# Last block's v repeated in float32, its z written to the buffer of p, and VectorE's scalar reads placed behind the issue of that z

## The chip, the cores and the metric

The kernel runs on one core of one Trainium2 chip. The metric is device time in microseconds (us) of one execution. Below, TensorE is PE in the rows (PEld are its weight loads), VectorE is DVE, ScalarE is ACT, GpSimd is POOL and SyncE is SP; DVEq is VectorE's sequencer, the part that reads registers and issues instructions.

## The reference

A graph layer over 53125 edges between 3125 nodes with 32 features each, and a layer norm of the sum:

```python
r = edge_vec / norm(edge_vec);  sh1 = sqrt(3) * r
xs, xd = x[edge_src], x[edge_dst]
s1 = concat(xs[:, :8], xd[:, :8]);  v1 = concat(xs[:, 8:], xd[:, 8:]) as (E, 16, 3)
w  = relu(emb @ fc1_w1) @ fc1_w2          # four (16, 8) matrices per edge
vdot1 = einsum('euk,ek->eu', v1, sh1) / sqrt(3)
s_t = a1 * (s1 . Wss + vdot1 . Wvv);  v_t = a1 * ((s1 . Wsv) sh1 + v1 . Wvs)
w2 = relu(emb @ fc2_w1) @ fc2_w2          # six (8, 8) matrices per edge
# the same once more with s_t, v_t and w2 gives scal, gates, vecs
edge_out = concat(tanh(scal), vecs * tanh(gates)) * edge_weight
x = layernorm(x + segment_sum(edge_out, dst))
```

The edges come sorted by destination, with many per node.

## The kernel before

The edges are padded and cut into NB = 104 blocks of BE = 512 edges, four tiles of 128. Blocks are counted from 0, so block 103 is the last. All engines run the same written-out loop `for i in STEPS` over i = -5 to 104; at step i each engine does one stage each for several blocks. The order of work on each engine is the order in which this loop is written, and semaphores order the engines against each other. There is no scheduler.

The stages that matter here, for a block k:

- `first_layer(k)` on TensorE: four float32 products, each over 32 rows, into PSUM banks 0 to 3 (line L1073 in the rows).
- `products(k)` on VectorE (L751): those four banks times the hidden layer `h1`, into the buffer `p_s`.
- `sum_1(k)` on TensorE (L986): four column groups of `v_ps` (bank 7) from `p_s`. It is v of this block.
- v is then split in three bfloat16 parts that sum to the float32 value, in place: ScalarE copies `v_ps` to the bfloat16 tile `v_s` (`part_of_v(k, 0)`, L528), TensorE takes the first of these away from the groups that hold later parts (`less_part(k, 0)`, L993), ScalarE copies again, TensorE again, ScalarE a third time. This way group 0, 1 and 2 of `v_s` come to hold the three parts.
- `repeat(k)` on TensorE (L1029): four bfloat16 products with the selection matrix `rep_m` repeat v into banks 0 to 3, each over 32 rows.
- `products2(k)` on VectorE (L791): those banks times the second hidden layer `h2`, into the buffer `z_s`.
- `sum_2(k)` on TensorE (L1004), a copy to `u_r` on ScalarE (`copy_u`, L500), and `turn(k)` on TensorE (L1053), four transposes into bank 7 (bank 0 for the last block).
- `gates(k)`, `gate_sums(k)` on VectorE (L802, L805, L807; L811, L814), `tanhs(k)` on ScalarE (L482), `gated(k)` and `outputs(k)` on VectorE (L773, L778), `over_nodes(k)` on TensorE (L1021), `accumulate(k)` on VectorE (L766).

`accumulate(k)` adds a window of 42 columns at an offset that is the block's first destination node. The offset is read from SBUF into a register of VectorE's sequencer by `base_of(k)` (L757); one such read is a TENSOR_LOAD, two register operations and an assertion. The flag of L852 (has any block more than a window of nodes) is read in the same way. In the loop there is one such read each step, written behind `products2`. Behind the loop VectorE's program reads

```python
            o, a, b, c, d = range(NB - 5, NB)
            flag = dve.value_load(misfits[0:1, 0:1], min_val=0, max_val=EP)
            bases_of = {k: base_of(k) for k in (o, a, b)}
            gated(a)
            outputs(a)
            gates(b)
            products2(d)
            gate_sums(b)
```

so o is block 99 and a, b, c, d are blocks 100 to 103. When all blocks are added, 16 products on TensorE take the mean away (L1159), and VectorE and ScalarE do the layer norm.

Of the kernel before, what the change touches and what calls it, by code (L numbers as in the profile page):

```python
# [9 lines left out]
ALU = mybir.AluOpType  # L10
# [37 lines left out]
def program(nc, xp, xt, src_t, dst_t, dst_rows, base_col, bases_row, emb, vec_t, wgt, w1, w2a, w2b, out):  # L48
    ctx = ExitStack()
    with ctx:  # L50
        def sb(name, shape, dt=F32):
            return ctx.enter_context(nc.sbuf_tensor(name, shape, dt))

        def sem(name):
            return ctx.enter_context(nc.semaphore(name))
# [16 lines left out]
        sel_g = sb("sel_g", [128, 4, 8])  # L72
        of_group = sb("of_group", [128, 4])
        of_part = sb("of_part", [128, 4])
        sum_m = sb("sum_m", [128, 4, 8])
        rep_m = sb("rep_m", [128, 4, 16, 8], BF16)
        less = [sb(f"less{n}", [128, 128], BF16) for n in range(2)]
# [35 lines left out]
        z_s = sb("z_s", [128, 4, BE])  # L113
        u_r = [sb(f"u{n}", [128, BE]) for n in range(2)]
        v_s = sb("v_s", [128, BE], BF16)
        m1 = sb("m1", [128, T, 4, 16])
        m2 = sb("m2", [128, T, 2, 16])
        gsc = sb("gsc", [128, T, 16])
# [73 lines left out]
        setup_step = sem("setup_step")  # L192
        consts_ready = sem("consts_ready")
        rep_step = sem("rep_step")
        misfit_parts = sem("misfit_parts")
        misfit_sum = sem("misfit_sum")
        misfits_ready = sem("misfits_ready")
# [69 lines left out]
        def real(m):  # L267
            return 0 <= m < NB
# [210 lines left out]
        def _(act):  # L479
# [109 lines left out]
            for i in STEPS:  # L589
                if real(i):  # L590
                    hidden_2(i)
                if real(i):
                    part_of_v(i, 0)
                if real(i + 1):
                    hidden_1(i + 1)
                if real(i):
                    part_of_v(i, 1)
                if i == -1:
                    act.wait_ge(n2_ready, 2)
                    nc.scalar.activation(nrm_t[:, TA:TILES], n2_t[:, TA:TILES], ACT.Sqrt).then_inc(norm_ready, 1)  # L600
                if real(i + 3) and i < 2:
                    copy_sources(i + 3)
                if real(i + 3):
                    copy_rows(i + 3)
                if real(i + 3) and i >= 2:
                    copy_sources(i + 3)
                if real(i + 4):
                    copy_one_hot(i + 4)
                if real(i + 4) and i + 4 >= 1:
                    copy_oht(i + 4)  # L610
                if real(i):
                    part_of_v(i, 2)
                if real(i - 3):
                    tanhs(i - 3)
                if real(i - 1):
                    copy_u(i - 1)
                if real(i + 2):
                    copy_f(i + 2)
                later_emb(i)
# [15 lines left out]
        def _(dve):  # L635
# [89 lines left out]
            link(nc.vector.tensor_reduce(of_group[:], ident[:].rearrange("p (g c) -> p g c", g=4), AX.X, ALU.add))  # L725
            link(nc.vector.tensor_reduce(of_part[:], ident[:].rearrange("p (g n c) -> p n g c", g=4, n=4), AX.XY, ALU.add))
            nc.vector.tensor_scalar(less[1][:], ident[:], of_part[:, 2:3], -1.0, ALU.mult, ALU.mult).then_inc(rep_step, 1)
            link(nc.vector.tensor_tensor(of_part[:, 0:1], of_part[:, 0:1], of_part[:, 1:2], ALU.add))
            link(nc.vector.tensor_tensor(of_part[:, 1:2], of_part[:, 1:2], of_part[:, 2:3], ALU.add))
            link(nc.vector.tensor_tensor(of_part[:, 0:1], of_part[:, 0:1], of_part[:, 2:3], ALU.add))  # L730
# [5 lines left out]
            def late_constants():  # L736

                dve.wait_ge(weights_loaded, 48)
                link(nc.vector.tensor_scalar(w_z[:], w_z[:], c2, None, ALU.mult))
                nc.vector.tensor_scalar(w_z[:, 0, 16:24], w_z[:, 0, 16:24], SQRT3, None, ALU.mult).then_inc(weights_ready, 1)  # L740
                nc.vector.tensor_copy(iota[:], iota_i[:]).then_inc(consts_ready, 1)
                dve.wait_ge(dst_loaded, 16)
                nc.vector.tensor_copy(dst_f[:], dst_i[:]).then_inc(place_ready, 1)
                nc.vector.memset(acc[:], 0.0).then_inc(acc_zeroed, 1)
                link(nc.vector.tensor_reduce(strip_sum[:], ident[:].rearrange("p (g c) -> p c g", g=4), AX.X, ALU.add))
                nc.vector.tensor_scalar(centre[:], strip_sum[:], -1.0 / D, None, ALU.add).then_inc(consts_ready, 1)

            def products(m):
                dve.wait_ge(g_done, m + 1)
# [38 lines left out]
            def products2(k):  # L788
                dve.wait_ge(rep_done, k + 1)
                dve.wait_ge(h2_ready, k + 1)  # L790
                nc.vector.tensor_tensor(z_s[:], ps[:, 0:4, :], h2_r[k % 3][:].unsqueeze(1).to_broadcast([128, 4, BE]),  # L791
                                        ALU.mult).then_inc(z_done, 1)

            def gates(k):
# [21 lines left out]
            for i in STEPS[:-1]:  # L816
                if real(i):
                    products(i)
                if real(i - 3):
                    gates(i - 3)  # L820
                if real(i - 1):
                    products2(i - 1)
                if real(i - 5):
                    base = base_of(i - 5)
                if real(i - 4):
                    gated(i - 4)
                if real(i - 5):
                    accumulate(i - 5, base)
                if real(i - 3):
                    gate_sums(i - 3)  # L830
                if real(i - 4):
                    outputs(i - 4)
                if real(i + 2):
                    sum_along(i + 2)
                if i == 0:
                    late_constants()

                for step, at_step in enumerate((-2, -2, 0, 0, 0, 1, 1, 1)):
                    if i == at_step:
                        if step >= 1 and step != 2:  # L840
                            dve.wait_ge(r4_step, step if step < 2 else step - 1)
                        ins = directions(step, TA, TILES)
                        if step == 1:
                            ins.then_inc(n2_ready, 1)
                        elif step == 7:
                            ins.then_inc(r4_ready, 1)
                        else:
                            ins.then_inc(r4_step, 1)


            o, a, b, c, d = range(NB - 5, NB)
            flag = dve.value_load(misfits[0:1, 0:1], min_val=0, max_val=EP)  # L852
            bases_of = {k: base_of(k) for k in (o, a, b)}
            gated(a)
            outputs(a)
            gates(b)
            products2(d)
            gate_sums(b)
            gates(c)
            gated(b)  # L860
            gate_sums(c)
# [73 lines left out]
        def _(pe):  # L935
# [59 lines left out]
            def sum_2(k):  # L995
                pe.wait_ge(z_done, k + 1)
                if k == 0:
                    pe.wait_ge(weights_ready, 4)
                    pe.wait_ge(consts_ready, 3)
                pe.wait_ge(h1_ready, min(k + 3, NB))  # L1000
                if k + 2 >= NB:
                    pe.wait_ge(u_ready, k)
                for g in range(4):
                    last = nc.tensor.matmul(s2_ps[32 * g:32 * g + 32], w_z[:, min(g, 1), :], z_s[:, g, :],  # L1004
                                            start=True, stop=True)
                last.then_inc(s2_done, 1)

# [17 lines left out]
            def repeat(k):  # L1025
# [4 lines left out]
                                            start=True, stop=True)  # L1030
                last.then_inc(rep_done, 1)

            def rows(m):
                pe.wait_ge(window_loaded[m % 3], 16 * (m // 3 + 1))
                pe.wait_ge(oht_copied, m + 1)
                if m == 1:
                    pe.wait_ge(rows_copied, 1)
                if m >= 2:
                    pe.wait_ge(f_copied, m - 1)
                for t in range(T):  # L1040
                    last = nc.tensor.matmul(rows_ps[:, t, :], oht_r[m % 2][:, TE * t:TE * t + TE], window_r[m % 3][:],  # L1041
                                            start=True, stop=True)
                last.then_inc(rows_done, 1)

            def turn(k):
                pe.wait_ge(u_ready, k + 1)
                bank = 0 if k == NB - 1 else 7
                if k < NB - 1:
                    pe.wait_ge(v_step, 3 * min(k + 3, NB))
                if 1 <= k < NB - 1:  # L1050
                    pe.wait_ge(e_free, k)
                for t in range(T):
# [40 lines left out]
            for i in STEPS:  # L1093
                if i == -4:
# [3 lines left out]
                    pe.wait_ge(misfits_ready, 1)  # L1098
                    flag = pe.value_load(misfits[0:1, 0:1], min_val=0, max_val=EP)
                    spread_places(0)  # L1100
                if real(i - 1):
                    repeat(i - 1)
                if real(i):
                    hidden_2(i)
# [10 lines left out]
                    pe.wait_ge(misfits_ready, 1)  # L1115
                if real(i + 1):
                    hidden_1(i + 1)
                if real(i):
                    less_part(i, 0)
                if real(i + 1):  # L1120
                    first_layer(i + 1)
                if real(i + 4) and i + 4 >= 1:
                    spread_places(i + 4)
                if real(i):
                    less_part(i, 1)
                if i == NB:
                    turn(i - 2)
                if real(i - 1):
                    sum_2(i - 1)
                if real(i - 2) and i < NB:  # L1130
                    turn(i - 2)
                if real(i + 2):
                    turn_features(i + 2)
# [82 lines left out]
```

## Time and profile before

| | |
|---|---|
| median of 3 runs | 744.84 us (744.56 to 747.78) |
| the profiled execution | 744.64 us, of which 742.8 us is the span of the trace |
| busy, share of the span | PE 93%, DVE 93%, ACT 75%, POOL 71% |
| chain that ended last | PE 87%, DVE 4% |

The span is counted from the first to the last instruction in the trace; 1.84 us of the execution lie around it. Times in the rows are us from the start of the span unless they say ns. "x8" is the number of instructions merged in a row; a float32 product counts as two. The bracket at the end of a timeline row gives the engine's idle time before it and what ended it.

### The profile page before, as it was taken

The numbers are of one execution on the slowest core, as the hardware profiler recorded it, in microseconds if no ns is written. First come the engines' busy times: TensorE is split into PE (matmuls) and PEld (weight loads), VectorE is DVE, ScalarE is ACT, GpSimd is POOL, SyncE is SP. The second block draws the span as 40 slices with busy tenths as digits, with TensorE's granted clock in tenths as the row PEclk, the third lists the DMA queues.
The fourth block names the chain that finished last, engine by engine and source line by source line (L and its number), as shares of the span: only waits on it lengthen the run. The fifth ranks groups of instructions, "written<-read, shape, count | busy, mean of one in ns | idle before, by whom it ended". The sixth has DMA issues, their size and how long they took to land.

```text
span 742.8 us, 19328 instructions
## 1 busy us (share of the span) xinstructions
PE 687.2 (93%) x5990; PEld 282.9 (38%) x5990; DVE 691.7 (93%) x1231; ACT 560.2 (75%) x1281; POOL 528.0 (71%) x653
## 2 busy tenths in 40 slices
PE   2359999999999999999999999999999999999984
PEld 2113334434443444344344444334434443444321
DVE  7488999999999999999999999999999999999986
ACT  3238887887888778888888888877788888878752
POOL 5676888778876887688768886787778876887200
PEclk7569999999999999999999999999999999999998
DMA  5412211111111211121112111211121111111000
GB/s 132 112 34 47 47 32 28 40 46 28 30 42 27 50 26 42 28 47 31 43 26 45 29 43 27 48 31 27 40 46 29 28 39 26 41 27 27 20 1 23
DMA packets 45822, 28.49 MB, mean 38 GB/s; under 512 B 23299, under 2 KB 43941, under 8 KB 45721
## 3 DMA queue, kind: packets, MB, share of 16 engines
q1 hardware_dynamic: 31402, 19.43, 9.9%
q0 software_dynamic: 13312, 6.84, 6.0%
q8 instruction: 52, 0.85, 0.5%
q10 hardware_dynamic: 1006, 0.96, 0.5%
q14 instruction: 50, 0.40, 0.2%
HBM read 22.46 MB, written 4.74 MB: 37 GB/s over the span
## 4 chain that ended last, share of the span: by engine, by line
PE 87%; DVE 4%; issue 2%; ACT 1%; POOL 1%; DVEq 0%; ACTq 0%
PE ps L1073 16%; PE ps L986 14%; PE ps L1004 13%; PE ps L993 9%; PE ps L1053 8%; PE ps L974 6%; PE ps L1029 5%; PE ps L1066 4%; PE ps L1060 3%; PE ps L964 3%; PE ps L1041 3%; PE ps L948 2%; PE ps L1021 2%; DVE p_s L751 2%; ACT v_s L528 1%
## 5 line engine op out<-in xcount | busy, mean ns | idle before, releaser
L374 POOL DMA_INDIRECT xs<-in_xp,src_i x416 | 401.0, 964 | 115.2 <-issue 104.3
L751 DVE TENSOR_TENSOR p_s<-ps,h 128x2048 f32<-128x2048 f32 x104 | 238.3, 2292 | 21.6 <-PE ps L1073 20.9
L791 DVE TENSOR_TENSOR z_s<-ps,h 128x2048 f32<-128x2048 f32 x104 | 237.6, 2284 | 1.3 <-PE ps L1029 1.2
L528 ACT CAST v_s<-ps 128x512 bf16<-128x512 f32 x312 | 182.2, 584 | 48.3 <-PE ps L986 43.2
L1073 PE MATMUL ps<-f,w_f 32*128 32x512 f32 x832 | 119.7, 642 | 4.3
L986 PE MATMUL ps<-p_s,sum_m 128*32 128x512 f32 x832 | 111.7, 605 | 0.6 <-DVE p_s L751 0.5
L1004 PE MATMUL ps<-z_s,w_z 128*32 128x512 f32 x832 | 110.8, 605 | 1.5 <-DVE z_s L791 1.5
L494 ACT COPY f<-ps 128x512 f32<-128x512 f32 x104 | 61.0, 587 | 41.9 <-PE ps L974 41.5
L993 PE MATMUL ps<-v_s,less 128*128 128x512 bf16 x208 | 81.1, 390 | 2.8 <-ACT v_s L528 2.6
L416 POOL TENSOR_TENSOR along<-fe,r 128x192 f32<-128x192 f32 x104 | 54.2, 521 | 32.8 <-ACT fe L506 26.3
L1053 PEld LDWEIGHTS ps<-ident,u 128*128 128x128 f32 x416 | 43.8, 141 | 87.6 <-issue 87.0
L534 ACT ACTIVATE h<-ps 128x512 f32<-128x512 f32 x104 | 62.2, 598 | 19.7 <-PE ps L1060 12.4
L540 ACT ACTIVATE h<-ps 128x512 f32<-128x512 f32 x104 | 62.2, 598 | 13.7 <-PE ps L1066 8.5
L488 ACT ACTIVATE oht<-ps 126x512 bf16<-126x512 f32 x104 | 62.5, 601 | 11.1 <-POOL e_part L397 5.3
L500 ACT COPY u<-ps 128x512 f32<-128x512 f32 x104 | 61.1, 588 | 12.4 <-PE ps L1004 2.1
L1053 PE MATMUL ps<-ident,u 128*128 128x128 f32 x416 | 68.0, 286 | 1.3 <-DVE m L807 1.0
L974 PE MATMUL ps<-ident,fe 128*128 128x128 f32 x416 | 63.5, 276 | 5.9 <-ACT ohs L523 5.7
L993 PEld LDWEIGHTS ps<-v_s,less 128*128 128x128 bf16 x208 | 19.9, 96 | 89.9 <-ACT v_s L528 78.5
L417 POOL TENSOR_TENSOR fe<-fe,r 128x192 f32<-128x192 f32 x104 | 54.0, 519 | 0.0
L974 PEld LDWEIGHTS ps<-ident,fe 128*128 128x128 f32 x416 | 49.2, 143 | 8.7 <-issue 7.3
L1021 PEld LDWEIGHTS ps<-ohs,eo_all 128*32 128x32 f32 x832 | 25.1, 108 | 68.0 <-issue 65.5
L1073 PEld LDWEIGHTS ps<-f,w_f 32*128 32x128 f32 x832 | 35.3, 185 | 34.2 <-issue 34.2
(129 smaller groups left out, 848.7 us busy)
## 6 DMA issues: line engine op xcount, KB each, us to landing
emb<-e_dram SPq DMA_DIRECT2D x309, 30.0 KB
xs<-in_xp,src_i POOLq DMA_INDIRECT x416
e_dram<-e_part SPq DMA_DIRECT2D x7, 360.0 KB, 3.0
e_in<-in_emb SPq DMA_DIRECT2D x8, 240.0 KB, 2.9
window<-x_dram SPq DMA_DIRECT2D x104, 7.9 KB
eo_all<-in_vec_t SPq DMA_DIRECT2D x1, 528.0 KB, 5.0
x_dram<-eo_all SPq DMA_DIRECT2D x1, 525.0 KB
place<-place_dram SPq DMA_DIRECT2D x26, 20.0 KB
```

The source lines that it names most:

```text
L374: nc.gpsimd.indirect_dma_start(xs_r[n][:, t, :], None, xp, bass.IndirectOffsetOnAxis(src_i[:, m * T + t:m * T + t + 1], axis=0)).then_inc( ...
L488: nc.scalar.activation(oht_r[m % 2][:], oht_ps, ACT.Relu).then_inc(oht_copied, 1)
L528: nc.scalar.copy(v_s[:], v_ps).then_inc(v_step, 1)
L534: nc.scalar.activation(h1_r[m % 2][:], h1_ps, ACT.Relu, scale=1.0 / math.sqrt(10.0)).then_inc(h1_ready, 1)
L751: nc.vector.tensor_tensor(p_s[:], ps[:, 0:4, :], h1_r[m % 2][:].unsqueeze(1).to_broadcast([128, 4, BE]), ALU.mult).then_inc(p_done, 1)
L791: nc.vector.tensor_tensor(z_s[:], ps[:, 0:4, :], h2_r[k % 3][:].unsqueeze(1).to_broadcast([128, 4, BE]), ALU.mult).then_inc(z_done, 1)
L974: last = nc.tensor.transpose(f_ps[:, TE * t:TE * t + TE], fe_r[m % 2][:, t].rearrange("p g c -> p (g c)"), ident[:])
L986: last = nc.tensor.matmul(v_ps[32 * g:32 * g + 32], sum_m[:].rearrange("p n c -> p (n c)"), p_s[:, g, :], start=True, stop=True)
L993: nc.tensor.matmul(v_ps, less[n][:], v_s[:], start=False, stop=True, skip_group_check=True).then_inc(s1_step, 1)
L1004: last = nc.tensor.matmul(s2_ps[32 * g:32 * g + 32], w_z[:, min(g, 1), :], z_s[:, g, :], start=True, stop=True)
L1053: last = nc.tensor.transpose(ps[:, bank, TE * t:TE * t + TE], u_r[k % 2][:, TE * t:TE * t + TE], ident[:])
L1073: last = nc.tensor.matmul(ps[:, g, :], w_f[32 * g:32 * g + 32], f_r[m % 2][32 * g:32 * g + 32], start=True, stop=True)
```

## The change

The constants get one more selection matrix, `rep_last`, in float32 (128 x 16 x 8). It is built in two steps: `first_copy` in VectorE's setup, and the broadcast of it in step 6 of the loop (`select_last`). For block 103 alone, ScalarE copies `v_ps` once, to the float32 tile `v_last`; the two further parts and the two `less_part` products fall away. `repeat(103)`, which stood at the start of step 104, is replaced by `repeat_last` in step 103: four float32 products with `rep_last` and `v_last`, behind `turn(101)` and ahead of `sum_2(102)`. Its result times `h2` goes to `p_s` in place of `z_s`. On VectorE, `gates(101)` and `products2(103)` move ahead of the four scalar reads, the reads stand right behind `products2(103)`, and `gated(100)` and `outputs(100)` behind the reads, with the first gate sum of block 101 between them.

```diff
@@ ScalarE
-                if real(i):
+                if i == NB - 1:
+                    act.wait_ge(s1_step, 3 * i + 1)
+                    nc.scalar.copy(v_last[:], v_ps).then_inc(v_last_copied, 1)
+                elif real(i):
                     part_of_v(i, 0)
...
-                if real(i):
+                if real(i) and i < NB - 1:
                     part_of_v(i, 1)
...
@@ VectorE
             nc.vector.tensor_scalar(less[1][:], ident[:], of_part[:, 2:3], -1.0, ALU.mult, ALU.mult).then_inc(rep_step, 1)
+            link(nc.vector.tensor_scalar(first_copy[:], sel_w[:], of_part[:, 0:1], None, ALU.mult))
...
+            def select_last():
+                dve.wait_ge(rep_step, 6)
+                nc.vector.tensor_copy(rep_last[:], first_copy[:].unsqueeze(1).to_broadcast([128, 16, 8])).then_inc(last_selected, 1)
...
-                nc.vector.tensor_tensor(z_s[:], ps[:, 0:4, :], h2_r[k % 3][:].unsqueeze(1).to_broadcast([128, 4, BE]),
+                z = p_s if k == NB - 1 else z_s
+                nc.vector.tensor_tensor(z[:], ps[:, 0:4, :], h2_r[k % 3][:].unsqueeze(1).to_broadcast([128, 4, BE]),
...
-            flag = dve.value_load(misfits[0:1, 0:1], min_val=0, max_val=EP)
-            bases_of = {k: base_of(k) for k in (o, a, b)}
-            gated(a)
-            outputs(a)
             gates(b)
             products2(d)
+            bases_of = {k: base_of(k) for k in (o, a, b)}
+            flag = dve.value_load(misfits[0:1, 0:1], min_val=0, max_val=EP)
+            gated(a)
             gate_sums(b)
+            outputs(a)
             gates(c)
@@ TensorE
+            def repeat_last():
+                pe.wait_ge(z_done, NB - 1)
+                pe.wait_ge(v_last_copied, 1)
+                pe.wait_ge(last_selected, 1)
+                for g in range(4):
+                    last = nc.tensor.matmul(ps[:, g, :], rep_last[32 * g:32 * g + 32].rearrange("p j c -> p (j c)"),
+                                            v_last[32 * g:32 * g + 32], start=True, stop=True)
+                last.then_inc(rep_done, 1)
...
             def turn(k):
-                if k < NB - 1:
-                    pe.wait_ge(v_step, 3 * min(k + 3, NB))
+                if k < NB - 3:
+                    pe.wait_ge(v_step, 3 * (k + 3))
+                elif k < NB - 1:
+                    pe.wait_ge(v_last_copied, 1)
...
-                if real(i - 1):
+                if real(i - 1) and i < NB:
                     repeat(i - 1)
...
-                if real(i):
+                if real(i) and i < NB - 1:
                     less_part(i, 1)
-                if i == NB:
+                if i >= NB - 1:
                     turn(i - 2)
+                if i == NB - 1:
+                    repeat_last()
                 if real(i - 1):
                     sum_2(i - 1)
-                if real(i - 2) and i < NB:
+                if real(i - 2) and i < NB - 1:
                     turn(i - 2)
```

What this makes of the order on TensorE, from the sum of v of block 103 (`ps<-p_s,sum_m`) to the sum of its z. Before:

```order
L986 MATMUL ps<-p_s,sum_m 32x512 x4
L1021 MATMUL ps<-ohs,eo_all 32x42 x4
L993 MATMUL ps<-v_s,less 128x512 x2
L1004 MATMUL ps<-z_s,w_z 32x512 x4
L1053 MATMUL ps<-ident,u 128x128 x4
L1029 MATMUL ps<-v_s,rep_m 128x512 x4
L1021 MATMUL ps<-ohs,eo_all 32x42 x4
L1053 MATMUL ps<-ident,u 128x128 x4
L1004 MATMUL ps<-z_s,w_z 32x512 x4
L1090 MATMUL ps<-xt_n,centre 32x400 x2
```

After; line numbers have moved, and `less_part` is gone, the transposes and the repeat of block 103 stand ahead of `sum_2(102)`, and the sum of its z reads `p_s`:

```order
L1002 MATMUL ps<-p_s,sum_m 32x512 x4
L1037 MATMUL ps<-ohs,eo_all 32x42 x4
L1080 MATMUL ps<-ident,u 128x128 x4
L1054 MATMUL ps<-v_last,rep_last 128x512 x4
L1020 MATMUL ps<-z_s,w_z 32x512 x4
L1037 MATMUL ps<-ohs,eo_all 32x42 x4
L1080 MATMUL ps<-ident,u 128x128 x4
L1020 MATMUL ps<-p_s,w_z 32x512 x4
```

So the products ahead of the repeat are now four transposes and no longer two `less_part`, the eight halves of `sum_2(102)` and the transposes.

On VectorE, from the last `outputs` of the loop (block 99) on, before:

```order
L778 TENSOR_TENSOR eo_all<-m_1,eo_all 128x4x3x8
L852 TENSOR_LOAD misfits
L852 ISA x2
L757 TENSOR_LOAD bases
L757 ISA x2
L757 TENSOR_LOAD bases
L757 ISA x2
L757 TENSOR_LOAD bases
L757 ISA x2
L773 TENSOR_TENSOR eo_all<-eo_all,wgt_s 128x4x16
L778 TENSOR_TENSOR eo_all<-m_0,eo_all 128x4x3x8
L802 TENSOR_TENSOR m<-ps,r 128x96
```

and after:

```order
L791 TENSOR_TENSOR eo_all<-m_1,eo_all 128x4x3x8
L816 TENSOR_TENSOR m<-ps,r 128x96
L819 TENSOR_TENSOR m<-ps,r 128x256
L821 TENSOR_TENSOR m_1<-m,ps 128x96
L805 TENSOR_TENSOR p_s<-ps,h_1 128x2048
L770 TENSOR_LOAD bases
L770 ISA x2
L770 TENSOR_LOAD bases
L770 ISA x2
L770 TENSOR_LOAD bases
L770 ISA x2
L871 TENSOR_LOAD misfits
```

The four reads (L852 and L757 before, L770 and L871 now) have moved from ahead of the gates of block 101 to behind the z of block 103 (`p_s<-ps,h_1` at L805), and `gated(100)` with them.

## Rows read from the trace of the kernel before

**Rows 1.** The page: the chain that ended last, and the costliest group of VectorE

```profile
PE 87%; DVE 4%; issue 2%; ACT 1%; POOL 1%; DVEq 0%; ACTq 0%
...
L751 DVE TENSOR_TENSOR p_s<-ps,h 128x2048 f32<-128x2048 f32 x104 | 238.3, 2292 | 21.6 <-PE ps L1073 20.9
```

**Rows 2.** By stretch: PE, PEld, DVE, ACT, POOL busy (count), TensorE's clock, DMA, GB/s

```profile
716.00:724.00 8.00, 5.61 (x55) 2.12 (x51) 5.85 (x14) 3.74 (x8) 0.00 (x0) 1.00 0.00 0
724.00:733.00 9.00, 5.91 (x68) 2.49 (x68) 7.11 (x26) 2.82 (x6) 0.00 (x0) 1.00 0.02 4
733.00:743.00 10.00, 1.66 (x18) 0.42 (x16) 4.42 (x12) 1.21 (x3) 0.00 (x0) 0.80 0.13 40
```

**Rows 3.** Timeline of TensorE, end of the kernel: start, us, instruction, idle before

```profile
713.81 1.14 PE L1073 MATMUL ps<-f,w_f 32*128 32x512 f32 x8
...
719.86 0.39 PE L993 MATMUL ps<-v_s,less 128*128 128x512 bf16 x1 [0.62 <-ACT v_s L528]
...
721.25 1.06 PE L1004 MATMUL ps<-z_s,w_z 128*32 128x512 f32 x8
722.25 0.66 PE L1053 MATMUL ps<-ident,u 128*128 128x128 f32 x4
722.84 0.40 PE L1029 MATMUL ps<-v_s,rep_m 32*128 32x512 bf16 x4
...
726.58 1.06 PE L1004 MATMUL ps<-z_s,w_z 128*32 128x512 f32 x8 [1.48 <-DVE z_s L791]
...
728.36 0.66 PE L1053 MATMUL ps<-ident,u 128*128 128x128 f32 x4
...
731.26 0.28 PE L1021 MATMUL ps<-ohs,eo_all 128*32 128x42 f32 x8 [1.15 <-DVE eo_all L778]
...
733.11 1.55 PE L1159 MATMUL ps<-acc,centre 128*32 128x400 f32 x16
```

**Rows 4.** Timeline of VectorE, end of the kernel

```profile
715.01 2.29 DVE L751 TENSOR_TENSOR p_s<-ps,h 128x2048 f32<-128x2048 f32 x1 [0.44 <-PE ps L1073]
...
717.87 2.28 DVE L791 TENSOR_TENSOR z_s<-ps,h 128x2048 f32<-128x2048 f32 x1
...
720.77 0.28 DVE L778 TENSOR_TENSOR eo_all<-m,eo_all 128x96 f32<-128x96 f32 x1
723.14 0.23 DVE L773 TENSOR_TENSOR eo_all<-eo_all,wgt_s 128x64 f32<-128x64 f32 x1 [2.08 <-issue]
723.40 0.29 DVE L778 TENSOR_TENSOR eo_all<-m,eo_all 128x96 f32<-128x96 f32 x1
723.58 0.25 DVE L802 TENSOR_TENSOR m<-ps,r 128x96 f32<-128x96 f32 x1
...
724.24 2.29 DVE L791 TENSOR_TENSOR z_s<-ps,h 128x2048 f32<-128x2048 f32 x1
726.44 0.28 DVE L811 TENSOR_TENSOR m<-m 128x128 f32<-128x128 f32 x1
...
728.15 0.29 DVE L778 TENSOR_TENSOR eo_all<-m,eo_all 128x96 f32<-128x96 f32 x1
...
729.39 0.26 DVE L802 TENSOR_TENSOR m<-ps,r 128x96 f32<-128x96 f32 x1 [0.87 <-PE ps L1053]
```

**Rows 5.** Timeline of ScalarE, end of the kernel

```profile
719.22 0.59 ACT L528 CAST v_s<-ps 128x512 bf16<-128x512 f32 x1 [0.52 <-PE ps L986]
```

**Rows 6.** VectorE's sequencer, the flag read, then a base read in the loop (durations in ns)

```profile
L852 DVEq TENSOR_LOAD <-misfits x1: 310/310/310, 720.6 to 720.6; - x1
...
L757 DVEq TENSOR_LOAD <-bases x1: 306/306/306, 717.8 to 717.8; - x1
```

**Rows 7.** Timeline of VectorE, in the setup

```profile
27.82 0.37 DVE L785 TENSOR_REDUCE fe<-along 128x64 f32<-128x192 f32 x1 [2.90 <-POOL fe L417]
```

**Rows 8.** In the setup: a stretch as in rows 2, and TensorE's timeline in it

```profile
34.00:36.00 2.00, 1.38 (x13) 0.93 (x17) 0.00 (x0) 0.88 (x2) 1.70 (x2) 0.50 0.17 26
...
35.49 2.09 PE L1073 MATMUL ps<-f,w_f 32*128 32x512 f32 x8
```

More of the change, by code:

```diff
@@ L74, in program @@
         of_part = sb("of_part", [128, 4])
+        first_copy = sb("first_copy", [128, 8])
         sum_m = sb("sum_m", [128, 4, 8])
@@ L115, in program @@
         v_s = sb("v_s", [128, BE], BF16)
+        v_last = sb("v_last", [128, BE])
+        rep_last = sb("rep_last", [128, 16, 8])
         m1 = sb("m1", [128, T, 4, 16])
@@ L194, in program @@
         rep_step = sem("rep_step")
+        last_selected = sem("last_selected")
+        v_last_copied = sem("v_last_copied")
         misfit_parts = sem("misfit_parts")
@@ L834, in _ @@
                     sum_along(i + 2)
+                if i == 6:
+                    select_last()
                 if i == 0:
@@ L1003, in sum_2 @@
                 for g in range(4):
-                    last = nc.tensor.matmul(s2_ps[32 * g:32 * g + 32], w_z[:, min(g, 1), :], z_s[:, g, :],
+                    last = nc.tensor.matmul(s2_ps[32 * g:32 * g + 32], w_z[:, min(g, 1), :], (p_s if k == NB - 1 else z_s)[:, g, :],
                                             start=True, stop=True)
@@ L1117, in _ @@
                     hidden_1(i + 1)
-                if real(i):
+                if real(i) and i < NB - 1:
                     less_part(i, 0)
@@ L1123, in _ @@
                     spread_places(i + 4)
-                if real(i):
+                if real(i) and i < NB - 1:
                     less_part(i, 1)
-                if i == NB:
+                if i >= NB - 1:
                     turn(i - 2)
+                if i == NB - 1:
+                    repeat_last()
                 if real(i - 1):
                     sum_2(i - 1)
-                if real(i - 2) and i < NB:
+                if real(i - 2) and i < NB - 1:
                     turn(i - 2)
```

## The prediction

> **What bounds the kernel now.** I read the page first. Its chain gives TensorE 87% of the span, and VectorE sat idle ahead of the product of `p_s` for 21.6 us over 104 blocks, 0.21 us a block, waiting for TensorE [rows 1]. So the loop runs at TensorE's pace, and the change takes nothing from the loop. It works on the last 25 us, which I read next in the table by stretch: from 716 to 733 us TensorE is busy 11.5 us of 17 and VectorE 13.0, so both wait for something [rows 2]. What for stands in the two timelines.
>
> On TensorE the three-part split of v of block 103 runs from 719.22, where ScalarE takes the first copy, and its products are spaced by ScalarE's copies (first `less_part` at 719.86) [rows 3, 5]. Then follow `sum_2(102)` at 721.25, the transposes of block 101 at 722.25 and the repeat at 722.84, over at 723.24 [rows 3]. But the z of block 103 starts only at 724.24 [rows 4]. VectorE is the later of the two: its last `outputs` of the loop starts at 720.77, and the next work at 723.14, with 2.08 us idle put down to issue [rows 4]. That is the four scalar reads: the first starts at 720.6 [rows 6], so they hold VectorE 723.14 - 720.6 = 2.5 us, or 0.62 us each. Behind them come `gated(100)`, `outputs(100)` and the gates of block 101, 1.10 us to the z. From the z on everything hangs on VectorE and on the way back over TensorE: sum of z at 726.58, transposes of block 103 at 728.36, `gates(103)` at 729.39 [rows 3, 4]. At that last place two more reads are in the way: they begin beside the `outputs` at 728.15, and 2 x 0.62 gives 729.39, the start seen [rows 4]. The row names TensorE as the releaser, but its transposes ended at 729.02 [rows 3]. From 729.39 to the end the program is the same before and after.
>
> **When z can start after the change, TensorE's side.** ScalarE's copy of `v_ps` to float32 has the shape of the copy at 719.22, which took 0.59 us whatever it writes here; I take 719.81. TensorE followed that copy at 719.86 [rows 3, 5]. Now the transposes of block 101 start there, and the repeat follows 722.84 - 722.25 = 0.59 us behind, at 720.45 [rows 3]. The four float32 products over 32 rows were never run at this place; `first_layer` is the same form (32x512, eight instructions). There VectorE started 715.01 - 713.81 = 1.20 us after the first of them [rows 3, 4]. So z can start at 721.65. The wait for the z of block 102 costs nothing: that z started at 717.87 and is over at 720.15 [rows 4].
>
> **VectorE's side.** `outputs(99)` starts at 720.77 and holds 0.18 us (723.40 to 723.58), the gates of a block hold 0.66 (723.58 to 724.24) [rows 4]: ready at 721.61. Both sides meet at 721.65, so neither a cheaper repeat nor cheaper gates alone would give more. z starts 724.24 - 721.65 = **2.59 us earlier**.
>
> **What the reads cost behind the issue of z.** In the loop a read stands right behind z: it starts at 717.8 with z at 717.87 [rows 4, 6], so reads run beside the product. The four take 2.5 us from 0.05 ahead of z's start. z gives way to its successor after 726.44 - 724.24 = 2.20 [rows 4]. VectorE goes on 2.45 after z's start, **0.25 us late**. If the reads fit entirely, this is 0; if they started only with z's end, it is 2.50 (a rival below). I take 0.25, since the row shows the overlap of one, and the other three are the same instructions.
>
> Where z has to wait for TensorE, the reads may start earlier than z. The Trainium skill (Perfetto Trace Analysis, DVE / Act Engine Instruction) says that the sequencer pushes an instruction into a wait queue and is then ready for the next. By that rule the reads would start at z's push and not at its start, and the sum would gain up to 0.25 more; by the row, which shows 0.07 us between them, it would not. The trace leaves it open, since nothing there waits long enough; the page is not used in the sum.
>
> **What is put between z and `gates(103)`.** `gated(100)` and `outputs(100)`, once ahead of z, now lie behind it. They held 723.58 - 723.14 = 0.44 us together [rows 4]: **0.44 us back**. With the first gate sum between them part of the gap is filled, so 0.3 is the lower bound. Their readers are `over_nodes(100)` on TensorE, behind the transposes of block 103, and those come later anyway.
>
> **What is late next.** `sum_2(102)` now stands behind the repeat, near 721.5 in place of 721.25. From a `sum_2` to its transposes is 728.36 - 726.58 = 1.78, so those of block 102 run from 723.3 to 723.95, and VectorE wants them for `gates(102)` at about 724.9. The sum of z of block 103 follows z's start by 726.58 - 724.24 = 2.34, at 723.99, just behind them; its transposes follow at 725.77 and end at 726.43 [rows 3]. `gates(103)` on VectorE's side comes at 729.39 - 2.59 + 0.25 + 0.44 = 727.49. So TensorE has 1.06 us to spare there, and VectorE with its reads is the bound of this stretch.
>
> **Edits at nothing.** `first_copy` is one small instruction in VectorE's setup, behind which VectorE idles 2.90 us for GpSimd [rows 7]; uncovered it would cost some 0.3. `select_last` is one copy in step 6, of about 0.2 us, against the 0.21 us that VectorE idles in a block [rows 1]; uncovered 0.2. Two copies less on ScalarE and two products less on TensorE free nothing beyond the times above. Writing z to `p_s` is the same instruction, and its reader `sum_1(103)` is done long before.
>
> **Sum.** -2.59 + 0.25 + 0.44 = -1.90. The profiled execution took 744.64, so 742.74; it lies 0.20 below the median of the runs, so the median to expect is **742.9**. The bounds: 2.3 us gained with the reads hidden and `outputs` at 0.3, some 0.95 gained with the repeat at its dearest row.
>
> **Rivals.**
> *The float32 repeat is dear, or another place holds the tail.* Products of this form took 2.09 us at 1.2 GHz [rows 8], 0.95 more than at 2.4. TensorE's clock was at full speed from 716 to 733 [rows 2] and now idles less ahead of the repeat, which speaks against; a switch of shapes that costs, or a tail bound that I do not see, would look the same. Gain 0.95, 743.9. Chance 0.14.
> *The reads are not hidden.* They start with z's end: 2.50 in place of 0.25, and the sum is -2.59 + 2.50 + 0.44 = +0.35: 745.2. For it: before, four in a row held the engine 2.5 us. Against: the single read in the loop starts beside z [rows 4, 6], and VectorE does not idle behind that z. Chance 0.06.
> *Slower: the clock falls.* TensorE waits for `outputs(102)` ahead of its last node products, 1.15 us before [rows 3]. Its transposes of block 103 now end 2.59 earlier and that `outputs` 1.90, so it waits about 1.8. If the clock fell to 1.2 GHz there, the work from 731.26 to 734.66 would take 3.4 us more: 744.84 + 3.4 - 1.9 = 746.3. It decides once over half of that work runs at 1.2. Against: the clock held 1.00 over an idle time of 1.48 us [rows 2, 3], and the mean of 0.80 from 733 to 743 means that it fell some 4 us before 743, at 739, over 4 us after TensorE's last product. The Trainium skill (TensorE: Matmul & The Clock Gate, The HAM clock gate) likewise has an idle TensorE drop to 1.2 GHz; no row here shows it at waits this short. Chance 0.05.
> *The change does nothing measurable*, since added constants or moved addresses cost in the loop what the end gives: 744.8. No row speaks for it. Chance 0.07.
>
> **How the numbers follow.** The forecast has 0.68: a gain of 1.4 to 2.4 us, so 742.4 to 743.4. The range of 8 in 10 is **741.8 to 744.8**: it takes in the dear repeat and the hidden reads, and allows for the runs' own spread, which reached from 0.28 below to 2.94 above the median before. Half a per cent, about what a measurement of this kernel can tell from no change, is 3.7 us. No case reaches 741.1 or 748.6; for what I have missed I leave 0.03 for faster and 0.03 for slower, and 0.94 lies within.
>
> **What would show it right or wrong.** From the first product of `sum_1(103)` on, z of block 103 should start 2.6 us earlier than before, and `gates(103)` should follow it by 5.15 + 0.69 = 5.84 us in place of 5.15. The first repeat product should stand 0.6 us behind the first transpose. The repeat should take 1.1 us; TensorE should not be the bound at `gates(103)`; no idle of more than 0.3 us should stand behind z; the clock should read 1.00 to 733. The loop should take the same time a block. A wrong prediction would come from a wait for the transposes of block 102, from the reads, or from the clock.

## The result, and the profile after

The changed kernel took 743.05 us (median of 14 runs), the kernel before 746.22 (14 runs, timed together); the ratio is 0.9961 with a 95% interval of 0.9943 to 0.998. That is 2.9 us of gain, with 1.5 to 4.3 inside the interval. One of the 14 runs, at 3282.67 us, was disturbed and is in no comparison; it does count in the median of 743.05, and the other 13 have 742.64. The profiled execution took 743.45 us, with a span of 741.6.

The two spans differ by 1.2 us, but that number mixes two things. The first product of the sum of v of block 103 starts at 718.10 before and at 718.87 after: the setup and the loop came out 0.77 us longer in this execution. To compare ends, count from that product; call it S. Before, z starts at S+6.14, `gates(103)` at S+11.29 and the span ends at S+24.70 [rows 3, 4]. After, these places are S+3.58, S+9.35 and S+22.73 (741.6 - 718.87). The end is 1.97 us shorter.

TensorE's timeline of after (start, us, instruction, idle before; L1054 is the new repeat, L1080 the transposes, L1020 the sums of z):

```profile
718.87 1.07 PE L1002 MATMUL ps<-p_s,sum_m 128*32 128x512 f32 x8
...
720.68 0.63 PE L1080 MATMUL ps<-ident,u 128*128 128x128 f32 x4 [0.67 <-issue]
721.24 1.14 PE L1054 MATMUL ps<-v_last,rep_last 32*128 32x512 f32 x8
722.31 1.06 PE L1020 MATMUL ps<-z_s,w_z 128*32 128x512 f32 x8
...
724.08 0.66 PE L1080 MATMUL ps<-ident,u 128*128 128x128 f32 x4 [0.63 <-ACT u L505]
724.79 1.07 PE L1020 MATMUL ps<-p_s,w_z 128*32 128x512 f32 x8
...
726.58 0.66 PE L1080 MATMUL ps<-ident,u 128*128 128x128 f32 x4
...
730.09 0.28 PE L1037 MATMUL ps<-ohs,eo_all 128*32 128x42 f32 x8 [1.36 <-DVE eo_all L791]
```

Where [rows 3] has the `less_part` products, the sum of block 102, the transposes and the repeat, there are now the transposes, from 0.11 us after ScalarE's one copy on (719.99 to 720.57), and 0.56 us behind them the float32 products. These take 1.14 us, as `first_layer` does.

VectorE's timeline of after (L805 is z, L816 the first instruction of `gates`, L786 `gated`, L791 `outputs`):

```profile
721.55 0.29 DVE L791 TENSOR_TENSOR eo_all<-m,eo_all 128x96 f32<-128x96 f32 x1
721.72 0.25 DVE L816 TENSOR_TENSOR m<-ps,r 128x96 f32<-128x96 f32 x1
...
722.45 2.29 DVE L805 TENSOR_TENSOR p_s<-ps,h 128x2048 f32<-128x2048 f32 x1
724.96 0.23 DVE L786 TENSOR_TENSOR eo_all<-eo_all,wgt_s 128x64 f32<-128x64 f32 x1 [0.22 <-issue]
...
728.22 0.26 DVE L816 TENSOR_TENSOR m<-ps,r 128x96 f32<-128x96 f32 x1 [0.87 <-issue]
```

The 2.08 us of idle time of [rows 4] are gone. z starts as soon as the gates of block 101 and the repeat are both done, and behind z only 0.22 us are idle. The chain shows that these are the reads (L770 a block's offset, L871 the flag; the first line is z, beside which the first load runs):

```profile
722.46 0.30 DVE p_s L805
...
722.80 0.19 DVEq L770
...
723.09 0.31 DVEq L770
...
723.71 0.30 DVEq L770
...
724.33 0.31 DVEq L871
...
724.89 0.02 DVEq L871
```

The four reads follow one behind the other: the last is over at 724.91, 2.46 us after z's start, and `gated(100)` starts at 724.96. TensorE's clock stayed at full speed to 731 us (columns as in rows 2):

```profile
718.00:724.00 6.00, 4.63 (x49) 1.83 (x49) 5.97 (x14) 2.00 (x4) 0.00 (x0) 1.00 0.00 0
724.00:731.00 7.00, 5.29 (x56) 1.97 (x56) 5.43 (x25) 2.60 (x6) 0.00 (x0) 1.00 0.00 1
```

### The profile page after: what moved, and what is told of

Same layout as the page of the kernel before. It is cut to its first block, busy times and chain, and to the rows that moved or that the text cites. A ratio compares the mean times of both kernels' runs of the same rounds, so it can differ in the third digit from the quotient of the medians.

```text
span 741.6 us, 19332 instructions
## 1 busy us (share of the span) xinstructions
PE 689.3 (93%) x5992; PEld 284.1 (38%) x5992; DVE 692.1 (93%) x1233; ACT 557.8 (75%) x1279; POOL 528.0 (71%) x653
## 4 chain that ended last, share of the span: by engine, by line
PE 87%; DVE 4%; issue 2%; ACT 1%; POOL 1%; DVEq 0%; ACTq 0%
PE ps L1100 16%; PE ps L1002 14%; PE ps L1020 13%; PE ps L1009 9%; PE ps L1080 8%; PE ps L990 6%; PE ps L1045 5%; PE ps L1093 4%; PE ps L1087 3%; PE ps L980 3%; PE ps L1066 3%; PE ps L964 2%; PE ps L1037 2%; DVE p_s L764 2%; ACT v_s L533 1%
## 5 line engine op out<-in xcount | busy, mean ns | idle before, releaser
L805 DVE TENSOR_TENSOR z_s<-ps,h 128x2048 f32<-128x2048 f32 x103 | 235.3, 2285 | 1.3 <-PE ps L1045 1.2
L1020 PE MATMUL ps<-z_s,w_z 128*32 128x512 f32 x824 | 109.7, 605 | 0.0
L1080 PEld LDWEIGHTS ps<-ident,u 128*128 128x128 f32 x416 | 43.6, 140 | 87.4 <-issue 86.0
L493 ACT ACTIVATE oht<-ps 126x512 bf16<-126x512 f32 x104 | 62.6, 602 | 11.3 <-POOL e_part L402 5.3
L1080 PE MATMUL ps<-ident,u 128*128 128x128 f32 x416 | 67.9, 286 | 1.7 <-issue 0.9
```

Of the source, the lines that this page charges most:

```text
L493: nc.scalar.activation(oht_r[m % 2][:], oht_ps, ACT.Relu).then_inc(oht_copied, 1)
L805: nc.vector.tensor_tensor(z[:], ps[:, 0:4, :], h2_r[k % 3][:].unsqueeze(1).to_broadcast([128, 4, BE]), ALU.mult).then_inc(z_done, 1)
L1080: last = nc.tensor.transpose(ps[:, bank, TE * t:TE * t + TE], u_r[k % 2][:, TE * t:TE * t + TE], ident[:])
```

## The experiments

All were timed against the kernel before on the same chip. "At S+" places are from each kernel's own profile.

**VectorE's order alone** (the kernel before, with this one edit):

```diff
-            flag = dve.value_load(misfits[0:1, 0:1], min_val=0, max_val=EP)
-            bases_of = {k: base_of(k) for k in (o, a, b)}
-            gated(a)
-            outputs(a)
             gates(b)
             products2(d)
+            bases_of = {k: base_of(k) for k in (o, a, b)}
+            flag = dve.value_load(misfits[0:1, 0:1], min_val=0, max_val=EP)
+            gated(a)
             gate_sums(b)
+            outputs(a)
```

> The kernel before with the new order of VectorE's end alone (gates 101 and z of block 103, then the four reads); the split in three bfloat16 parts and TensorE's order stay. All places are counted from S, the first product of the sum of v of block 103 (before: z at S+6.14, gates of block 103 at S+11.29, end of the span at S+24.70; after: S+3.58, S+9.35, S+22.73). Theory 1, both parts are needed: VectorE is free at S+2.85 but has to wait for the transposes of block 101, over at S+4.81; gates 0.66, z at S+5.5; with the reads 0.3 over and gated and outputs behind it, gates of 103 at S+11.3: no gain, end S+24.7. Theory 2, the reads were all of it: most of the 1.97 us comes here, end near S+22.8. Theory 3, the repeat was all of it: also no gain, but then the next kernel has the 1.97.

Measured: ratio 1.0012 (0.9997 to 1.0026). z at S+5.51, `gates(103)` at S+11.00, the end at S+25.92. The reason is in VectorE's timeline of this kernel:

```profile
722.02 0.26 DVE L802 TENSOR_TENSOR m<-ps,r 128x96 f32<-128x96 f32 x1 [1.89 <-PE ps L1053]
...
722.69 2.28 DVE L791 TENSOR_TENSOR z_s<-ps,h 128x2048 f32<-128x2048 f32 x1
724.91 0.23 DVE L773 TENSOR_TENSOR eo_all<-eo_all,wgt_s 128x64 f32<-128x64 f32 x1
```

VectorE now idles 1.89 us for the transposes, which still stand behind the split. So the reads were not all of it. The end came 1.2 us later than expected, although `gates(103)` came 0.3 earlier; that is the clock, which was at 1.00 up to 731.1 and at 0.50 from 731.2 to 734.6. The last products on TensorE took 2.61 us in place of the 1.55 of [rows 3]:

```profile
732.42 2.61 PE L1159 MATMUL ps<-acc,centre 128*32 128x400 f32 x16
```

**The float32 repeat alone** (the changed kernel, with VectorE's lines put back in the order of before, the diff above reversed).

> The changed kernel with VectorE's end in the order of before (reads, gated, outputs, gates 101, z); the float32 copy and repeat stay. Theory 1: the repeat is done at S+3.6 but VectorE comes to z at S+6.14 as before, because reads and what follows them hold it; gates of 103 at S+11.3, no gain, end S+24.7. Theory 3: end near S+22.8. Theory 2: no gain. If this and the order alone both give nothing, the 1.97 us is the product of the two. If the timed ratio is still below 0.998 here, part of the ratio 0.9961 comes from the setup or the loop, not from the end.

Measured: ratio 1.0008 (0.999 to 1.0026). The repeat starts at S+2.36 and z at S+6.13. Each half of the change alone moves the timed result by nothing that can be told; z gains 0.63 from the one and 0.01 from the other, and 2.56 from both. `gates(103)` came at S+12.96, not S+11.3, and the end at S+26.39. TensorE's timeline of this kernel shows why:

```profile
717.71 1.06 PE L1002 MATMUL ps<-p_s,sum_m 128*32 128x512 f32 x8
...
720.07 1.14 PE L1054 MATMUL ps<-v_last,rep_last 32*128 32x512 f32 x8
...
726.18 1.93 PE L1020 MATMUL ps<-p_s,w_z 128*32 128x512 f32 x8 [1.48 <-DVE p_s L805]
...
729.52 1.11 PE L1080 MATMUL ps<-ident,u 128*128 128x128 f32 x4
```

The sum of z takes 1.93 us in place of 1.06, and the transposes 1.11 in place of 0.66: the granted clock is 0.50 here, which is 1.2 GHz. It fell at 725.7, in the wait of 1.48 us. This was not in my expectation.

**Everything but float32** (order of after on all engines, but the split in three parts kept; the conditions that leave out its second and third part for block 103 are taken away as well):

```diff
-                if i == NB - 1:
-                    act.wait_ge(s1_step, 3 * i + 1)
-                    nc.scalar.copy(v_last[:], v_ps).then_inc(v_last_copied, 1)
-                elif real(i):
+                if real(i):
                     part_of_v(i, 0)
...
             def repeat_last():
                 pe.wait_ge(z_done, NB - 1)
-                pe.wait_ge(v_last_copied, 1)
-                pe.wait_ge(last_selected, 1)
+                pe.wait_ge(v_step, 3 * NB)
                 for g in range(4):
-                    last = nc.tensor.matmul(ps[:, g, :], rep_last[32 * g:32 * g + 32].rearrange("p j c -> p (j c)"),
-                                            v_last[32 * g:32 * g + 32], start=True, stop=True)
+                    last = nc.tensor.matmul(ps[:, g, :], rep_m[32 * g:32 * g + 32, g].rearrange("p j c -> p (j c)"),
+                                            v_s[32 * g:32 * g + 32], start=True, stop=True)
```

> The changed kernel with everything but float32: the order on all engines is that of after, but v of block 103 is split in three bfloat16 parts and repeated from them. Theory 1: the third copy is over at S+3.85, the transposes of block 101 run behind it to S+4.55, gates to S+5.25, z at S+5.3; gates of 103 at S+11.05, end S+24.4, a gain of 0.25 of the 1.97. Rival, the float32 products as dear as the split they replace: z at S+3.6 to S+4, end S+22.7 to S+23.2.

Measured: ratio 0.999 (0.9969 to 1.0012), z at S+5.35. That is 1.77 us later than with float32. The price of the split is its two further copies on ScalarE with their products, not the repeat: the float32 repeat is the longer one (1.14 us against 0.40 in [rows 3]). The clock fell here too, at 721.8, before z: the transposes ahead of the gates took 0.70 us in place of 0.63, so under 0.1 of the 1.77 is the clock. Behind z it made `gates(103)` late, at S+12.39.

**The reads spread** (the changed kernel; two more reads behind the z of block 101, two behind that of block 102, and only those for blocks 102 and 103 behind the last z):

```diff
                 if real(i - 5):
                     base = base_of(i - 5)
+                if i == NB - 2:
+                    bases_of = {k: base_of(k) for k in (NB - 5, NB - 4)}
+                if i == NB - 1:
+                    bases_of[NB - 3] = base_of(NB - 3)
+                    flag = dve.value_load(misfits[0:1, 0:1], min_val=0, max_val=EP)
...
-            bases_of = {k: base_of(k) for k in (o, a, b)}
-            flag = dve.value_load(misfits[0:1, 0:1], min_val=0, max_val=EP)
+            bases_of.update((k, base_of(k)) for k in (c, d))
             gated(a)
...
             accumulate(o, bases_of[o])
-            bases_of.update((k, base_of(k)) for k in (c, d))
```

> The changed kernel with VectorE's six last reads spread: two more behind the z of block 101, two more behind that of block 102, and only the two of blocks 102 and 103 behind the last z; none ahead of gates 103. Theory 1 (VectorE with its reads bounds from z to gates 103, TensorE has about 1 us to spare): three reads (1.86 us) fit behind a z of 2.20, the first work behind z comes at z+2.20 in place of z+2.51, and gates of 103 at S+8.45, bound by TensorE's transposes; 0.9 us gained over after, end S+21.8. Rival (TensorE already is the bound at gates 103, or reads cannot run beside a product when there are several): gates of 103 stay at S+9.35, or the loop's last steps get 0.6 us longer each.

Measured: 741.36 us (6 runs, 740.83 to 741.65), ratio 0.9951 (0.9932 to 0.997). The first work behind z comes at z+2.20, `gates(103)` at S+8.40, the end at S+21.72, 1.01 before after's. VectorE's timeline:

```profile
717.46 2.28 DVE L805 TENSOR_TENSOR z_s<-ps,h 128x2048 f32<-128x2048 f32 x1
719.66 0.21 DVE L786 TENSOR_TENSOR eo_all<-eo_all,wgt_s 128x64 f32<-128x64 f32 x1
...
721.26 2.29 DVE L805 TENSOR_TENSOR p_s<-ps,h 128x2048 f32<-128x2048 f32 x1
723.46 0.21 DVE L786 TENSOR_TENSOR eo_all<-eo_all,wgt_s 128x64 f32<-128x64 f32 x1
...
726.08 0.26 DVE L816 TENSOR_TENSOR m<-ps,r 128x96 f32<-128x96 f32 x1 [0.24 <-PE ps L1083]
```

The three reads behind the z of block 102 (717.46) do not show: `gated` follows at 2.20. At `gates(103)` the last row has TensorE's transposes as the releaser, and this time it is true, since no read is left there. The program is the fastest of all that ran.

The next three kernels were executed once each (743.84, 744.03 and 748.0 us, against 744.09 for one execution of the kernel before), so only the places in their profiles are read.

**The transposes behind the sum again** (the changed kernel):

```diff
-                if i >= NB - 1:
+                if i == NB:
                     turn(i - 2)
                 if i == NB - 1:
                     repeat_last()
...
-                if real(i - 2) and i < NB - 1:
+                if real(i - 2) and i < NB:
                     turn(i - 2)
```

> The changed kernel with one piece of TensorE's order undone: the transposes of block 101 stand behind the sum of block 102 again, so the repeat of block 103 comes first. Counted from S as above. Theory 1 (two sides meet at z): the repeat runs from S+2.1 to S+3.2, the sum to S+4.2, the transposes to S+4.85, VectorE's gates 101 to S+5.5, z at S+5.55 in place of S+3.58; gates of 103 at S+11.3, end S+24.7: the whole gain is gone. Rival (z follows the repeat alone): z at S+3.3, a gain of 0.3 more.

Measured: z at S+5.53, `gates(103)` at S+11.03, the end at S+24.40, with the clock at 1.00. The float32 products start 0.26 us earlier than in after, yet z comes 1.95 later, because it needs the gates of block 101 and these need the transposes. The gain at the end shrinks to 0.30.

**The repeat twice** (`for g in (0, 1, 2, 3, 0, 1, 2, 3)` in `repeat_last`).

> The changed kernel with the four float32 products of the repeat run twice (same result). Theory 1: TensorE's side of z gets 1.05 us longer and VectorE has no slack there, so z at S+4.6, gates of 103 at S+10.4, end S+23.8. Rival (the bound is VectorE's side, TensorE has room): z moves by less than 0.5. If four of them take over 1.3 us here, they are dear in this place.

Measured: z at S+4.43, `gates(103)` at S+10.21, the end at S+23.63. Twice the products cost 0.85 at z and 0.90 at the end, so what is added to TensorE's side arrives almost in full. z has a wait of 0.85 us here:

```profile
721.91 0.25 DVE L821 TENSOR_TENSOR m<-m,ps 128x96 f32<-128x96 f32 x1
723.00 2.29 DVE L805 TENSOR_TENSOR p_s<-ps,h 128x2048 f32<-128x2048 f32 x1 [0.85 <-PE ps L1054]
725.51 0.23 DVE L786 TENSOR_TENSOR eo_all<-eo_all,wgt_s 128x64 f32<-128x64 f32 x1 [0.21 <-issue]
```

```profile
L770 DVEq TENSOR_LOAD <-bases x1: 302/302/302, 723.0 to 723.0; - x1
```

The first read starts with z, at 723.0, though z had been next in line since 722.15. In the kernel with the order alone, z did not wait for TensorE's repeat (it was over at 722.31), and the first read started at 722.43, 0.26 ahead of z at 722.69. There the work behind z came at z+2.22; here and in after it came at z+2.51.

**The reads twice** (the two lines with the four reads behind `products2(d)` written twice).

> The changed kernel with the four reads behind the last z done twice, eight in all. Theory 1 (the reads run beside z one after the other, 0.62 us each, and VectorE's next work waits for the last): first work at z+5.0 in place of z+2.51, gates of 103 at S+11.85, end S+25.2. Rival (the sequencer's reads overlap each other or fill a queue): less than 1.5 us more.

Measured: the next work at z+4.96, 2.45 us more for four more reads: serial, 0.61 each. `gates(103)` at S+11.80. The end came at S+27.91, 2.7 later than expected, with TensorE's clock at half from 729.5 us on.

**Again: before, after, the reads spread, the repeat alone** (no edit). Four ends had by then been longer than the arithmetic, each with a fall of the clock.

> The kernel before, unchanged, as a look at how far two executions of one program differ. In four of the seven profiles so far TensorE's clock fell to half within the last 25 us, in places where the engine had waited 1.4 to 2.3 us, and the end of the span then lay 1.2 to 2.7 us later than the arithmetic gives. Theory 4, a fall there is a matter of chance for any of these kernels whose TensorE waits in the end, and before is among them: the ratio to itself is 1.000 within 0.002, z at S+6.14, and gates of 103 at S+11.3 unless the clock falls there. Theory 1 alone: the same places, and end at S+24.7.

> The changed kernel, unchanged, once more. Theory 1: z at S+3.58 and gates of 103 at S+9.35, end S+22.7 with the clock at 1.00; ratio 0.9973 (1.97 us). Theory 4, the rest of the first ratio of 0.9961 (2.9 us) is that the clock falls less often in its end: the ratio stays near 0.996 again. If it comes out at 0.998, the surplus was noise.

> The version with the six reads spread, once more, since its six runs lay within 0.8 us where before spreads over 8. Theory 1: end at S+21.7, 2.98 us before that of before and 1.0 before that of after, ratio 0.996. Theory 4: ratio 0.9945 to 0.995, and a spread as narrow as that of after's better runs, unless the clock in the setup widens it.

> The version with the float32 repeat and VectorE's order of before, once more for its end. In its first profile the clock fell ahead of the sum of z of block 103, and gates of 103 came at S+12.96. Theory 4: with the clock at 1.00 there, gates of 103 at S+11.3 and end at S+24.7; z at S+6.13 either way. Rival, this order makes the clock fall every time: S+12.96 again.

Measured: before to itself 0.9999 (0.9982 to 1.0016); after 743.6 us, ratio 0.9964 (0.9946 to 0.9982); reads spread 741.38 us (6 runs), ratio 0.9935 (0.9913 to 0.9956); repeat alone 744.86 us, one run. The places before `gates(103)` came out within 0.02 us of those of the first profiles. The ends did not: before at S+26.37 in place of S+24.70, after at S+25.29 in place of S+22.73, reads spread at S+21.78, repeat alone at S+26.26. TensorE of the kernel before, second profile:

```profile
725.90 1.94 PE L1004 MATMUL ps<-z_s,w_z 128*32 128x512 f32 x8 [1.48 <-DVE z_s L791]
...
729.24 1.11 PE L1053 MATMUL ps<-ident,u 128*128 128x128 f32 x4
```

and of after, second profile, with the clock of two stretches:

```profile
728.92 0.28 PE L1037 MATMUL ps<-ohs,eo_all 128*32 128x42 f32 x8 [1.37 <-DVE eo_all L791]
729.13 1.52 PE L1117 MATMUL ps<-xt_n,centre 32*32 32x400 f32 x4
...
732.03 2.90 PE L1188 MATMUL ps<-acc,centre 128*32 128x400 f32 x16
```

```profile
726.00:728.00 2.00, 1.34 (x25) 0.52 (x24) 1.12 (x6) 0.19 (x1) 0.00 (x0) 1.00 0.00 0
...
730.00:732.00 2.00, 2.00 (x14) 1.13 (x12) 0.20 (x1) 0.10 (x1) 0.00 (x0) 0.50 0.04 8
```

In before the clock fell in the wait for z, at 725.0 (1.48 us, the same wait as in [rows 3], where it did not fall). In after it was at 1.00 up to 729.1 and at 0.50 from 729.2, 0.3 us behind the end of the wait for `outputs(102)` (1.37 us, 1.36 in the first profile, where it did not fall). The same program with the same waits meets both. The fall cost 1.67 us in the one and 2.56 in the other.

**The wait ahead of the last node products filled** (the changed kernel with `keep_warm(4)`, four float32 products on the identity, ahead of `over_nodes(NB - 2)`; they compute nothing that is used).

> The changed kernel with the idle time of TensorE ahead of the node products of block 102 filled: eight halves of float32 128x128 products on the identity (about 1.3 us of the 1.36 us waited there), into a PSUM bank that nobody reads any more. They compute nothing that is used. With the clock at 1.00 the end is that of after, S+22.7, so the fastest runs stay at 741.2 to 742. In the second profile of after the clock fell at this wait, between 728 and 730 us, and the end came at S+25.3. Theory 4, the spread of after (741.2 to 745.8) is largely this fall: no run in the upper group, median near 742.1, ratio 0.9945 to 0.995. Rival, the spread is made in the setup: median 743.0 to 743.6 and the same upper group, ratio 0.996 to 0.9965.

Measured: 975.15 us, against 978.68 for the kernel before in the same comparison, ratio 0.9959 (0.9931 to 0.9986). Every run of both kernels on that chip was some 230 us longer than elsewhere, with a mean clock of 0.87 to 0.90 in place of 0.96 to 0.97; why is not known. The wait was filled (0.32 us of it left) and the clock stayed up in the end, which took 22.72 us from S. But the question, whether the spread of after narrows, can't be read off runs that differ by ten microseconds for another reason. It stays open.

## Why the prediction was right, point by point

- **z can start 2.59 us earlier, both sides meeting there.** Measured 2.56. The transposes one way later cost 1.95 at z, the repeat made longer cost 0.85, the split kept cost 1.77, VectorE's order put back 2.55. All four pieces hold z; none of them alone frees it. That the two sides meet shows in z itself: it follows the last of the gates by 0.24 us (722.21 to 722.45) in place of 0.17 before, so it waits 0.07 for TensorE.
- **The float32 repeat costs what `first_layer` costs.** 1.14 us, as assumed. The rival of a dear repeat is ruled out.
- **The reads are hidden but for 0.25 us.** 0.31: z's successor comes at z+2.51 and not z+2.20. The rival of reads that are not hidden, which would have put it at z+4.7, is ruled out. The small miss is in where the first read starts: with z, not ahead of it, when z waits for TensorE. The page of the Trainium skill that I weighed there (Perfetto Trace Analysis, DVE / Act Engine Instruction) would, as I read it, have had the reads go ahead of a waiting z; the kernel with the repeat twice shows z waiting 0.85 us and its first read at z's own start, so the measurement decides against that for reads.
- **`gated` and `outputs` give 0.44 back.** All that was put between z and `gates(103)` came to 5.77 - 5.15 = 0.62, of which 0.31 is the reads; so 0.31 and not 0.44. The lower bound named for it was the better value: -2.56 + 0.31 + 0.31 = -1.94, which is what `gates(103)` moved.
- **TensorE has 1.06 us to spare at `gates(103)`.** Its transposes there end at 726.58 + 0.66 = 727.24, and `gates(103)` starts at 728.22: 0.98. The spread reads turn this into 0.95 us of gain at `gates(103)` and meet TensorE.
- **Sum -1.90, 742.9 us.** The end is 1.97 shorter in the pair of profiles whose clock did not fall: here the mechanism and its size hold. That the median, 743.05, lies 0.15 us from the forecast is luck. The forecast stands on a base of 744.84, the median of three runs; the fourteen have 746.22, 1.38 more. And the medians differ by 3.17, 1.27 more than the sum. The two misses cancel.
- **Setup and loop at nothing.** From the sum of v of one block to that of the next the step of the copy took 6.69 us in either kernel (80.22 to 86.91 before, 80.78 to 87.47 after). From there to S it is 631.19 before and 631.40 after. Of the 0.77 us by which the first profile of after was late at S, 0.56 stood by 80 us, so it arose mostly in the setup. The second profiles have S at 717.43 before and 717.71 after. Over all thirteen profiles S lies between 716.74 and 718.87, whatever the kernel, so a cost of some 0.3 us in the setup is neither shown nor excluded.
- **The clock falls: chance 0.05, since it held over 1.48 us idle.** This step was wrong. One profile in which it held told nothing of the next one. It fell within the last 26 us, with products still to run, in seven of the thirteen profiles other than the last experiment's, one of before and one of after among them. As a rival that decides between the two kernels it did not come true, since both pay it; as a property of this kernel's end it should have had even odds. Its sizes were too large as well: the wait for `outputs(102)` was 1.36 us and not 1.8, since the node products ahead of it start 2.27 us earlier and not 2.59 (they wait 0.21 for VectorE themselves), and the fall behind it cost 2.56 and not 3.4.

The timed ratios (0.9961 and 0.9964) are 0.7 to 0.9 us more than the 1.97 us of the end, which is 0.9974. Both intervals still hold 0.9974. For the spread reads, 2.98 us from the places would be 0.9960; the first interval holds it, the second ends just below, at 0.9956.

The mean granted clock of each run hints at where the surplus comes from. It was 0.969 or 0.970 in the six profiles without a fall and 0.961 to 0.967 in the seven with one. Splitting the runs at 0.967 is an estimate, since a late fall can hide at that value and the setup counts too. By it, 42 of 64 runs of before had a fall (two chips, 0.965 or less), 11 of 25 of after, and at most 1 of 12 with the reads spread. Among the runs without a fall the medians are 743.98 before and 741.89 after, 2.09 apart; among those with one 746.60 and 744.86, 1.74 apart. So within each group the gain is close to the 1.97 of the profiles, and the surplus fits a difference in how often the clock falls. For the reads spread (1 of 12 against 42 of 64) that difference is far beyond chance; their 12 runs lie between 740.64 and 742.10. For the change itself (11 of 25 against 42 of 64) it may still be chance, and that stays open.

## What to carry to other kernels

When one instruction waits for two engines that are late by about the same, moving either side alone shows nothing; work out both sides of the wait before dropping an edit as useless. A scalar read into a register of an engine's sequencer (0.61 us here) stops everything behind it but runs beside the instruction ahead of it. So place it behind the longest one, as many as fit in that one's length (three of them, 1.86 us, did not show behind a z of 2.20; four showed as 0.31). And where an end of a kernel has waits of over a microsecond on TensorE, compare places in the timeline, not totals, and look at more than one profile.

## What the runs showed of the hardware

- TensorE's clock fell to 1.2 GHz in this end in some executions and held in others of the same program. In three of the seven profiles with a fall it came inside a wait of 1.48 us (the second profile of before, both of the repeat alone). In the other four the engine was already busy again, 0.3 to 1.2 us behind a wait of 0.72 (split kept), 1.37 (the second profile of after), 1.38 (order alone) or 2.26 us (reads twice). A fall lengthened the end by 1.2 to 2.7 us, against the 1.97 that the change gives.
- Reads behind a VectorE instruction that waits for a semaphore start when that instruction starts (723.0 and 723.00), and 0.26 us ahead of it when it only waits for the engine (722.43 and 722.69).
- A chip was met on which the kernel before takes 978.68 us and not some 746; the ratio of the version with the filled wait to it was 0.9959 there.
